# Eleven of the fourteen NF4 additions of a piece as accumulating SBUF to SBUF DMAs issued by GpSimd

## What is computed

```python
def nf4_quant_dequant(w):
    flat = w.reshape(-1, BLOCKSIZE)                      # 64
    absmax = jnp.max(jnp.abs(flat), axis=1, keepdims=True)
    normalized = flat / jnp.where(absmax == 0, 1.0, absmax)
    bounds = (NF4_CODE[:-1] + NF4_CODE[1:]) * 0.5
    idx = jnp.searchsorted(bounds, normalized)
    return (NF4_CODE[idx] * absmax).reshape(shape)

def reference(x, Wq, Wk, Wv, Wo, w1, w2, w3):            # x (2, 1024, 512), 32 heads of 128, 8 kv heads
    x = x + _layernorm(attention(_layernorm(x), Wq, Wk, Wv, Wo))
    dq1, dq2, dq3 = (nf4_quant_dequant(w) for w in (w1, w2, w3))
    z = _layernorm(x)
    h = jax.nn.silu(z @ dq1.T) * (z @ dq2.T)             # 1376 wide
    return x + _layernorm(h @ dq3.T)
```

## Time and profile before

| | us |
|---|---|
| median of 2 runs | 1960.97 (1960.5 to 1961.45) |
| the profiled execution | 1959.31 |
| its span | 1957.5 |
| PE busy | 1876.3 (96%) |
| DVE busy | 1433.4 (73%) |
| POOL busy | 1235.9 (63%) |
| ACT busy | 1229.4 (63%) |
| POOL, the 416 additions of L488 | 534.3 |
| POOL, the 32 additions of L484 | 40.8 |

### The profile page before, as it was taken

One profiled execution on the slowest core, in us unless ns is written; L12 is line 12 of the kernel. 1 busy time (PEld: TensorE's weight loads), 2 busy tenths in 40 slices (PEclk: granted clock), 3 DMA queues, 4 the chain that ended last, 5 costly groups with the idle time before them and its releaser, 6 DMA issues.

```text
span 1957.5 us, 42161 instructions
## 1 busy us (share of the span) xinstructions
PE 1876.3 (96%) x11698; PEld 1252.8 (64%) x11698; DVE 1433.4 (73%) x3926; ACT 1229.4 (63%) x4840; POOL 1235.9 (63%) x1150
## 2 busy tenths in 40 slices
PE   4999999999999999999999999999989979999997
PEld 3667677777777777776777676777666635444443
DVE  6998888888888888888888888888899644302022
ACT  5777777777777777777777777776666535312121
POOL 3777777777777777777777777777677521212121
PEclk8999999999999999999999999999999989999999
DMA  5000000000000000000000000000100042000000
GB/s 199 25 26 25 26 25 24 24 24 24 32 25 24 24 24 24 29 24 24 24 24 24 30 29 24 24 24 13 54 13 7 7 134 79 26 1 22 0 21 21
DMA packets 44353, 61.43 MB, mean 31 GB/s; under 512 B 4928, under 2 KB 18496, under 8 KB 44288
## 3 DMA queue, kind: packets, MB, share of 16 engines
q1 hardware_dynamic: 44288, 60.64, 9.6%
HBM read 47.97 MB, written 12.65 MB: 31 GB/s over the span
## 4 chain that ended last, share of the span: by engine, by line
PE 62%; DVE 16%; issue 14%; POOL 3%; ACT 2%; DVEq 1%; DMA 0%; SPq 0%; POOLq 0%; ACTq 0%
PE bank L1250 18%; PE bank L1239 8%; PE bank L1278 6%; PE bank L1221 4%; PE bank L1294 4%; PE bank L1315 4%; PE bank L1379 3%; PE bank L1287 3%; DVE f_s L963 2%; PE bank L1205 2%; PE bank L1304 2%; POOL hl L527 2%; DVE f_nrm L953 2%; PE bank L1270 1%; PE bank L1297 1%
## 5 line engine op out<-in xcount | busy, mean ns | idle before, releaser
L488 POOL TENSOR_TENSOR f_acc<-f_acc,f_s 128x512 f32<-128x512 f32 (+1 forms) x416 | 534.3, 1284 | 30.6 <-POOL f_acc L488 0.4
L1250 PE MATMUL bank<-wh,xh 128*128 (+2 forms) x1024 | 334.9, 327 | 7.3 <-DVE cumh L1099 6.2
L1250 PE MATMUL bank<-wl,xh 128*128 (+2 forms) x1024 | 335.0, 327 | 0.0
L1250 PE MATMUL bank<-wh,xl 128*128 (+2 forms) x1024 | 334.7, 327 | 0.0
L469 POOL TENSOR_TENSOR pr<-pr,rp 128x512 f32<-128x512 f32 x128 | 133.0, 1039 | 229.5 <-DVE rp L894 229.5
L963 DVE TENSOR_SCALAR f_s<-f_nrm 128x512 f32<-128x512 f32 (+1 forms) x480 | 240.9, 561 | 3.7
L575 ACT ACTIVATE qe<-bank,nqm 128x128 f32<-128x128 f32 x512 | 180.8, 365 | 80.3 <-DVE qs L823 57.2
L527 POOL TENSOR_TENSOR hl<-hf,hh 128x512 f16<-128x512 f32 (+1 forms) x44 | 50.8, 1155 | 283.7 <-ACT hh L754 283.7
L1379 PE MATMUL bank<-xh,w 128*128 (+3 forms) x704 | 224.8, 382 | 3.8 <-ACT sg L748 3.8
L603 ACT ACTIVATE pr<-bank,pmx 128x128 f32<-128x128 f32 x512 | 180.9, 367 | 37.5 <-DVE pmx L887 29.6
L1239 PE MATMUL bank<-wh,oT 128*128 (+1 forms) x512 | 194.0, 379 | 3.8 <-DVE xl L1019 1.4
(11 more groups left out here) (177 smaller groups left out, 4973.7 us busy)
## 6 DMA issues: line engine op xcount, KB each, us to landing
f_raw<-wf SPq DMA_DIRECT2D x30, 256.0 KB, 2.6
dequantised<-f_dq SPq DMA_DIRECT2D x30, 256.0 KB, 2.0
wt<-dequantised SPq DMA_DIRECT2D x30, 256.0 KB, 3.0
raw_qkv<-wq SPq DMA_DIRECT2D x29, 256.0 KB, 2.5
raw_o<-wo SPq DMA_DIRECT2D x29, 256.0 KB, 2.6
rows<-x SPq DMA_DIRECT2D x4, 1024.0 KB, 9.3
xr<-x SPq DMA_DIRECT2D x16, 256.0 KB, 3.6
out<-yo SPq DMA_DIRECT2D x16, 256.0 KB, 2.1
```

The lines of the kernel that those rows point to most:

```text
L488: nc.gpsimd.tensor_tensor(f_acc[:, 0:w], f_acc[:, 0:w], f_s[:, k % 8, 0:w], ALU.add)\
L1250: last = nc.tensor.matmul(dst, av, w[:, sl + c, lo:hi], start=(n == 0), stop=(n == 3 * NC - 1))
```

## The change

POOL still makes two additions of terms, k = 1 into `f_acc[0]` (terms 0 and 1) and k = 3 into `f_acc[1]` (terms 2 and 3). Each of the terms 4 to 14 is added by a DMA that POOL issues, from the ring buffer onto `f_acc[k % 2]` in SBUF with `accum_op=ALU.add`: the even k (six) form one chain, the odd k (five) the other. A DMA of a chain is issued only when the one before it has landed (semaphores `f_even`, `f_odd`, 16 a DMA); the first ones, k = 4 and 5, wait for the addition into their sum. The waits stand on a small POOL instruction ahead of each DMA, an addition of one column into `f_gate`. In POOL's turn p = 0, behind `softmax_p` and ahead of `split_low`, the new function `nf4_join` waits for both chains and adds the two sums. DVE's waits before it writes over a ring buffer now go by the landing of the DMA that read it, and `nf4_end` by the join.

```diff
             def nf4_add(t):
                 w = width_of(t.i)
+                i = t.i
                 for k in NF4_STEPS[t.p]:
-                    pool.wait_ge(s["f_sd"], t.i * 15 + (k + 1))
-                    if k == 1:
-                        if not (isinstance(t.i, int) and t.i == 0):
-                            pool.wait_ge(s["f_dqd"], t.i)
-                        nc.gpsimd.tensor_tensor(f_acc[:, 0:w], f_s[:, 0, 0:w], f_s[:, 1, 0:w], ALU.add)\
+                    if k in (1, 3):
+                        pool.wait_ge(s["f_sd"], i * 15 + (k + 1))
+                        if k == 1 and not (isinstance(i, int) and i == 0):
+                            pool.wait_ge(s["f_dqd"], i)
+                        nc.gpsimd.tensor_tensor(f_acc[k // 2][:, 0:w], f_s[:, k - 1, 0:w], f_s[:, k, 0:w], ALU.add)\
                             .then_inc(s["f_ad"], 1)
-                    elif k > 1:
-                        pool.wait_ge(s["f_ad"], t.i * 14 + (k - 1))
-                        nc.gpsimd.tensor_tensor(f_acc[:, 0:w], f_acc[:, 0:w], f_s[:, k % 8, 0:w], ALU.add)\
-                            .then_inc(s["f_ad"], 1)
+                    elif k > 3:
+                        n = (k - 4) // 2
+                        pool.wait_ge(s["f_sd"], i * 15 + (k + 1))
+                        if n == 0:
+                            pool.wait_ge(s["f_ad"], i * 3 + (k - 3))
+                        else:
+                            pool.wait_ge(s["f_even"] if k % 2 == 0 else s["f_odd"],
+                                         i * (96 - k % 2 * 16) + 16 * n)
+                        nc.gpsimd.tensor_tensor(f_gate[:, k:k + 1], keep[:, 0:1], keep[:, 0:1], ALU.add)
+                        nc.gpsimd.dma_start(f_acc[k % 2][:, 0:w], f_s[:, k % 8, 0:w], accum_op=ALU.add)\
+                            .then_inc(s["f_even"] if k % 2 == 0 else s["f_odd"], 16)
+
+            def nf4_join(t):
+
+                i, w = t.i, width_of(t.i)
+                pool.wait_ge(s["f_even"], i * 96 + 96)
+                pool.wait_ge(s["f_odd"], i * 80 + 80)
+                nc.gpsimd.tensor_tensor(f_acc[0][:, 0:w], f_acc[0][:, 0:w], f_acc[1][:, 0:w], ALU.add)\
+                    .then_inc(s["f_ad"], 1)
...
                     nf4_add(l1)
                     softmax_p(l1)
+                if l1.real() and l1.p == STEP - 1:
+                    nf4_join(l1)
...
                 for k in NF4_STEPS[t.p]:

-                    if k >= 8:
-                        dve.wait_ge(s["f_ad"], i * 14 + max(k - 8, 1))
+                    if k >= 12:
+                        n = k - 12
+                        dve.wait_ge(s["f_odd"] if n == 1 else s["f_even"], i * (96 - k % 2 * 16) + (16 + n // 2 * 16))
+                    elif k >= 8:
+                        dve.wait_ge(s["f_ad"], i * 3 + (1 + (k - 8) // 2))
                     elif not (isinstance(i, int) and i == 0):
-                        dve.wait_ge(s["f_ad"], i * 14 - (6 - k if k < 7 else 0))
+                        left = (0, 48, 32, 32, 16, 16, 0, 0, 48)[k + 1] if k < 7 else 48
+                        dve.wait_ge(s["f_even"] if k % 2 == 0 else s["f_odd"],
+                                    i * (96 - k % 2 * 16) - left)
...
-                dve.wait_ge(s["f_ad"], i * 14 + 14)
+                dve.wait_ge(s["f_ad"], i * 3 + 3)
```

More of the change, by code:

```diff
@@ L188, in layer @@
         f_nrm = sb("f_nrm", [P, NF4_MAX])
-        f_acc = sb("f_acc", [P, NF4_MAX])
+        f_acc = [sb(f"f_acc{j}", [P, NF4_MAX]) for j in range(2)]
+        f_gate = sb("f_gate", [P, 16])
         f_dq = sb("f_dq", [P, NF4_MAX])
@@ L248, in layer @@
             x_st x_mv x_var x_ln x_rs x_shift x_norm x_turned x_hi x_lo zeroed id_in
-            f_in f_maxd f_safed f_recd f_nrmd f_sd f_ad f_dqd f_out""".split()
+            f_in f_maxd f_safed f_recd f_nrmd f_sd f_ad f_even f_odd f_dqd f_out""".split()
         s = {n: sem("s_" + n) for n in names}
@@ L521, in _ @@
             nf4_add(last_turn)
+            nf4_join(last_turn)
             def low_hidden(g, c):
@@ L971, in nf4_end @@
                 nc.vector.scalar_tensor_tensor(
-                    out=blocks(f_dq, w), in0=blocks(f_acc, w), scalar=float(CODE[0]),
+                    out=blocks(f_dq, w), in0=blocks(f_acc[0], w), scalar=float(CODE[0]),
                     in1=f_max[:, i % 2, 0:w // BLK].unsqueeze(2).to_broadcast([P, w // BLK, BLK]),
```

## The result

The changed kernel takes 2007.13 us (2005.74 to 2008.53, 2 runs) against 1960.97: 1.024 times as long (interval 1.022 to 1.026), +46 us. Its profiled execution has a span of 2006.7 us against 1957.5. The forecast was 2057, +96 us, in a range of 1945 to 2200: side and mechanism came true, the size was twice too large.

The account below looks back on a forecast made before the run. POOL's waits for DMA landings over two turns, 29.9 us against 26.04 of room, make PE wait for `qc`: 74 us in the loop, 8 outside, 12 hold-ups, 2 tail, 96 in all; 2057 us, range 1945 to 2200.

Parts of the forecast that it names:

- L: Time from the start of an accumulating DMA's issue on POOL to its landing, put at 4.0 us, between 2.0 and 5.8.
- 3g + 2L + d: POOL's DMA stretch in turn p = 3: three one-column gates of 0.2 us, two landings, one issue; 9.5 us instead of 6.74.
- d: POOL's own time in issuing one DMA, put at 0.9 us, between 0.33 and 1.27.
- the second reading: Part of the landing time: an accumulating transfer reads twice 256 KB, which was to add 0.8 us.
- 3.1 + 0.5 us a piece: Loss per loop piece: 3.1 us net from POOL's late `qc`, plus 0.5 us of mutual hold-ups between POOL's issues and `f_s`.
- Hold-ups of issues and `f_s`, 12 us: POOL's DMA issues and DVE's `f_s` delay each other, 0 to 1 us a piece, taken as 0.5, 12 us in all.
- The rival of held-off descriptors: DVE's `f_s` holds up POOL's descriptor writing: 41 or 101 us more, 2098 or 2158; chance 0.15, shared with landings above 5 us.
- The eight outside pieces, 8 us: Pieces outside the loop, whose turns carry other work, lose between 0 and 3.1 us each, taken as 1, 8 us.
- 8 + 2: Loss outside the loop: 8 us in the eight outside pieces, 2 us in the tail, where the last four additions become longer.
- The clock: PE's granted clock stays at 1.00 through waits of 1 to 3 us; it falls only with waits of 7 us or more.
- the second case: Rival that landings are short enough: the two turns take 24.4 us by the skill's estimate, PE never waits; chance 0.24.
- Landings short (0.24): Rival: landings below 3.0 us, break-even at 3.1, keep POOL on time; 1942 to 1985 us, chance 0.24.

Follow-up runs that it names:

- e4: The changed kernel with each DMA also waiting for the landing of the one before it in the other chain, one in flight instead of two: 2486.88 us, ratio 1.269.
- e2: The changed kernel with each of the eleven DMAs adding only the first half of the columns: 1953.07 us, ratio 0.997.
- e3: The changed kernel with the eleven DMAs copying the term onto the sum instead of adding it: 1948.53 us, ratio 0.995.
- e10: The changed kernel with POOL's join moved behind `qe` in turn p = 1 and DVE's `f_dq` behind the low decay: 1962.79 us, ratio 1.0015.
- e14: The changed kernel with DVE's `f_nrm` moved to the end of `nf4_blocks`, right behind `f_rec`, and nothing else: 2070.86 us, ratio 1.057.

## Why the prediction was right in side and wrong in size

- **What bounds the kernel, and the mechanism: right.** POOL's sum over two turns against PE's room decides, and PE waits at the transpose of `qc` at the end of p = 0. e4 (longer), e2 and e3 (shorter) bear it out on both sides, and e10, which takes the join out of that sum, removes the wait.
- **The step that failed is the size of L in the terms 3g + 2L + d.** For p = 3, first gate to `pr`, they gave 0.6 + 8.0 + 0.9 = 9.5 us. Measured from 1039.76 to 1047.56 are 7.80: 0.40 for the three gates, 3.42 and 3.37 for the landings, up to the gate that each releases, 0.61 for the last issue. So L was 3.4 and not 4.0, and d 0.6 and not 0.9. Of L, e3 shows which part was wrong: the plain copy was put at 3.2 us (the load's 2.6 less 0.33 plus 0.9) and took 2.3, the second reading at 0.8 and took 1.0. Why the copy is shorter no run shows. The starting figure was a load from DRAM, and the addition of its parts took for granted that issue and transfer don't overlap.
- **In p = 0 two errors met, by luck.** First gate to the join's end was put at 10.77 us and took 10.26. There the chain runs through the second DMA of a pair: 4.50 us from its issue to the next gate, then 3.47 for the last one, together the forecast's 2L = 8.0. That a second DMA takes about 1 us longer was not in the sum, and it hid that a DMA alone takes 3.4.
- **Not in the sum: `qc` held by `f_dq`,** 1.71 instead of 1.27 us. Both turns with it took 27.97 us instead of 29.9. With L = 3.4 in its place the prediction's own formula gives 27.55.
- **Why 2 us of sum are 50 of the time.** The room takes 26.04 us off either sum: 3.9 us of forecast delay, 1.9 of measured. A difference of two large numbers carries their errors whole. Against the forecast of 3.1 + 0.5 us a piece stand 1.13 measured (47.93 - 46.80).
- **Hold-ups of issues and `f_s`, 12 us: not between these two.** `f_s` has a mean of 0.436 us, and the landings keep their length from piece to piece; e14's longer ones have another cause. The rival of held-off descriptors has no place in the loop. But the engines do hold each other: `qc` loses 0.44 us a piece to `f_dq`, about 11 us over the loop. So the term's size was near by luck, and it lay between other operations. The Trainium skill (SBUF — State Buffer, "SBUF: two separate sides") speaks of a pair of ports that both engines share: of a GpSimd operation and a VectorE one that has two SBUF inputs or runs in a two-port mode, the one that starts first has the pair for its whole length, and the other waits. The rows agree in both directions: `f_s`, `f_dq` and `f_safe` wait for POOL's operation at hand, and `qc` (1.71 us) waits for `f_dq`.
- **The eight outside pieces, 8 us: too small.** The first four alone took 11.5 more (the loop starts at 245.94 instead of 234.42), 34.6 came in the loop, 3.1 behind it: 49.2 of span. Up to 246 us PE has the same wait for `qc`, seven times and 2.2 us in the mean. So the loop lost 34.6 us where the forecast had 74 + 12, and what lies outside it 14.6 where it had 8 + 2.
- **The clock: wrong.** I claimed that waits of 1 to 3 us leave it at 1.00. After a wait of 1.73 us at 823.40 it did not:
```profile
814.00:823.40 9.40, 7.67 (x54) 5.29 (x52) 8.59 (x27) 5.25 (x25) 6.68 (x9) 1.00 0.60 117
823.40:830.00 6.60, 6.60 (x30) 4.68 (x31) 2.75 (x9) 4.02 (x16) 2.58 (x3) 0.74 0.09 33
```
  In the second row the granted clock is 0.74, a mean of the two levels, with PE busy throughout. It happened in 3 of 24 pieces, 1.7 us each, 5 us of the 34.6.
- **The Trainium skill's estimate of 2.6 us** for a DMA issued by GpSimd (DMA: Bandwidth & Descriptors, "Anatomy of one DMA — SWDGE (gpsimd) path"): the plain copy of e3 took 2.3, the accumulating one 3.3. The prediction calls it a figure for plain copies; the section itself names no kind of DMA. It was nearer to the copy than my sum of parts; for the accumulating DMA it was 0.7 too short, and the second case, which rested on it, didn't come.
- **Landings short (0.24)** came nearer than I gave it credit for: L, at 3.4, was 0.3 above its break-even, and e2 with 2.7 and e3 with 2.3 came out at 1953 and 1949, inside that case's 1942 to 1985.

## What to carry to other kernels

When an engine hands work to DMAs, add up what it waits for between two deadlines of the engine it serves, and place the last wait (here the join) where nothing urgent queues behind it: the same eleven transfers cost 46 us or, with the join and `f_dq` moved, 4. Then look at what shares SBUF with the moved operation, at what the freed buffer's next load collides with, at which operation stands next in line, and at whether the moved one's inputs are ready, for the moves that made things worse went wrong in these ways. A landing has no single length: here 3.3 us alone and 4.1 to 4.4 as the second of a pair or beside a load, so put it into a sum by its place in the chain.
